# Shared FFN steps of the last tiles moved behind the constant tiles' indices

## What is computed

```python
def _ffn(x, gw, uw, dw):
    return jax.nn.silu(x @ gw.T) * (x @ uw.T) @ dw.T
shared = _ffn(xf, shared_gate, shared_up, shared_down)      # 704 hidden features, every token
probs = jax.nn.softmax(xf @ gate_w.T, axis=-1)
topw, topi = jax.lax.top_k(probs, 2)                        # 2 of 8 experts for each token
topw = topw / (topw.sum(-1, keepdims=True) + 1e-20)
routed = sum over experts of _ffn(xf, expert) * the token's weight for it
x = x + _layernorm(attention(_layernorm(x)))
x = x + _layernorm(shared + routed)
```

## Time and profile before

| | us |
|---|---|
| three runs, median (lowest to highest) | 841.98 (841.88 to 842.23) |
| the profiled execution, its own time | 840.84 |
| its span | 839.1 |
| TensorE busy in it | 783.3 |
| VectorE busy | 588.7 |
| ScalarE busy | 487.4 |
| GpSimd busy | 277.0 |

### The profile page before, as it was taken

How to read it: one execution, slowest core, us unless ns; L and a number is a source line. 1 busy time by engine, 2 the same in 40 slices (tenths; PEclk the granted TensorE clock), 3 DMA queues, 4 the chain that set the end, 5 groups by cost and what they waited for, 6 DMA issues and landing times.

```text
span 839.1 us, 21195 instructions
## 1 busy us (share of the span) xinstructions
PE 783.3 (93%) x6686; PEld 642.8 (77%) x6695; DVE 588.7 (70%) x1568; ACT 487.4 (58%) x1073; POOL 277.0 (33%) x301
## 2 busy tenths in 40 slices
PE   6989999999999997778999999999999999999990
PEld 3547777777777776666888888888888888888880
DVE  5758989898989898897888644555555555555552
ACT  3364848484857576533466655565656565656561
POOL 3011010101010101002565555555555555555542
PEclk9999999999999999999999999999999999999996
DMA  4114444444444343203264567856464646464633
GB/s 194 51 36 172 113 145 114 145 122 153 119 148 129 132 115 130 45 14 90 53 171 77 98 70 72 123 96 131 76 152 72 148 69 151 74 147 68 147 39 94
DMA packets 102708, 90.11 MB, mean 107 GB/s; under 512 B 63776, under 2 KB 94240, under 8 KB 101472
## 3 DMA queue, kind: packets, MB, share of 16 engines
q1 hardware_dynamic: 87664, 68.45, 28.7%
q0 software_dynamic: 14976, 20.78, 17.5%
HBM read 48.70 MB, written 27.39 MB: 91 GB/s over the span
## 4 chain that ended last, share of the span: by engine, by line
PE 73%; DVE 15%; issue 5%; ACT 5%; POOL 1%; DMA 1%; ACTq 0%; DVEq 0%; POOLq 0%
PE ps L948 41%; PE ps L963 19%; PE ps L1067 4%; PE ps L1099 3%; DVE wgu L1355 3%; DVE hf L1295 2%; PE ps L1061 2%; ACT wgu L805 2%; DVE wdn L1355 1%; DVE st L1537 1%; DVE att L1462 1%; PE ps L1028 1%; DVE hT L1305 1%; DVE st L1275 1%; PE ps L1070 1%
## 5 line engine op out<-in xcount | busy, mean ns | idle before, releaser
L948 PE MATMUL ps<-xhl,wgu 128*128 128x256 f16 x3102 | 383.6, 273 | 7.0 <-DVE hf L1295 5.2
L948 PEld LDWEIGHTS ps<-xhl,wgu 128*128 (+1 forms) x3102 | 301.8, 98 | 50.4 <-DVE hf L1295 6.8
L1295 DVE SCALAR_TENSOR_TENSOR hf<-ps,sc,silu 128x256 f32<-128x256 f32 x330 | 159.7, 484 | 172.4 <-ACT silu L755 146.2
L963 PE MATMUL ps<-wdn,hT 128*128 (+1 forms) x1870 | 253.3, 273 | 11.3 <-DVE hT L1305 8.5
L755 ACT ACTIVATE silu<-ps,sc 128x256 f32<-128x256 f32 x275 | 130.0, 473 | 226.2 <-PE ps L948 223.0
L963 PEld LDWEIGHTS ps<-wdn,hT 128*128 128x128 f16 x1870 | 180.9, 98 | 38.0 <-DVE hT L1305 7.6
L696 POOL DMA_INDIRECT acc_d<-ysb,gst x78 | 128.6, 1649 | 44.5 <-POOL gst L692 30.9
L641 POOL TENSOR_TENSOR rstd<-ve,mhalf 128x4 f32<-128x4 f32 (+1 forms) x32 | 30.7, 959 | 294.2 <-DVE ve L1280 272.5
L769 ACT CAST hT<-hf 128x256 f16<-128x256 f32 x275 | 109.7, 399 | 12.1 <-DVE hf L1295 10.1
L1305 DVE TENSOR_TENSOR hT<-hf,hT 128x256 f16<-128x256 f32 x275 | 114.8, 417 | 1.7
L685 POOL DMA_INDIRECT attw<-xn_d,gst x74 | 75.9, 1025 | 42.1 <-POOL gst L681 30.9
(11 more groups left out here) (242 smaller groups left out, 775.3 us busy)
## 6 DMA issues: line engine op xcount, KB each, us to landing
wgu<-in_gu SPq DMA_DIRECT2D x8, 1408.0 KB, 6.2
att<-in_x SPq DMA_DIRECT2D x16, 512.0 KB, 5.6
wdn<-in_dn SPq DMA_DIRECT2D x8, 768.0 KB, 8.2
x_d<-att SPq DMA_DIRECT2D x8, 512.0 KB, 2.9
xn_d<-wgu SPq DMA_DIRECT2D x8, 512.0 KB, 3.4
acc_d<-ysb SPq DMA_DIRECT2D x16, 256.0 KB, 3.3
att<-x_d SPq DMA_DIRECT2D x8, 512.0 KB, 4.8
att<-acc_d SPq DMA_DIRECT2D x7, 512.0 KB
```

Source lines behind the costliest of these rows:

```text
L948: ins = te.matmul(o, slot_gu(slot, hw, k, j), x(hx, k), start=(n == 0), stop=(n == len(TERMS) - 1))
L963: ins = te.matmul(y_bank(u, tt), h(hh), slot_dn(slot, c, hw), start=(c == 0 and n == 0 and tt == 0), stop=(c == FC - 1 and n == 1 and tt = ...
L1295: v.scalar_tensor_tensor(out=hf[lo:P, c % 2 * TW:(c % 2 + 1) * TW], in0=up, scalar=scale_of(slot, 1, lo, P), in1=silu[lo:P, c % 2 * TW:(c ...
```

## The change

Only the list `TAIL` is changed, the order of its steps. Nothing is added or taken away. Before, the H steps 5, 6 and 7 stood each behind a pair of `one_lo` steps or behind `one_hi` 1, all ahead of `route_indices`. Now `one_lo` 2 to 7 and `one_hi` 1 stand together, H 5 is behind `one_hi` 1, and H 6 and 7 are behind `route_indices`. D 4, G 7, D 5 and G 8 move behind the inversions with them. The heart of the diff:

```diff
-        ("G", 7), ("H", 6), ("D", 5), ("invert", 2), ("invert", 3), ("one_lo", 6), ("one_lo", 7), ("one_hi", 1), ("G", 8), ("H", 7),
...
+        ("G", 6), ("invert", 2), ("invert", 3), ("one_lo", 6), ("one_lo", 7), ("one_hi", 1), ("H", 5), ("invert", 4), ("invert", 5), ("invert", 6), ("invert", 7),
+        ("route_indices", 0), ("D", 4), ("G", 7), ("H", 6), ("D", 5), ("G", 8), ("H", 7), ("D", 6), ("G", 9), ("H", 8), ("D", 7), ("route_counts",), ("G", 10),
```

More of the change, by code:

```diff
@@ L82 @@
         ("H", 2), ("D", 1), ("route_slots", 1), ("one_lo", 1), ("route_weights", 1), ("G", 4), ("H", 3), ("D", 2), ("route_positions", 1), ("one_hi", 0),
[2 rows of a table removed]
-        ("invert", 4), ("invert", 5), ("invert", 6), ("invert", 7), ("route_indices", 0), ("D", 6), ("G", 9), ("H", 8), ("D", 7), ("route_counts",), ("G", 10),
+        ("G", 5), ("H", 4), ("D", 3), ("one_lo", 2), ("one_lo", 3), ("invert", 0), ("invert", 1), ("one_lo", 4), ("one_lo", 5),
+        ("G", 6), ("invert", 2), ("invert", 3), ("one_lo", 6), ("one_lo", 7), ("one_hi", 1), ("H", 5), ("invert", 4), ("invert", 5), ("invert", 6), ("invert", 7),
+        ("route_indices", 0), ("D", 4), ("G", 7), ("H", 6), ("D", 5), ("G", 8), ("H", 7), ("D", 6), ("G", 9), ("H", 8), ("D", 7), ("route_counts",), ("G", 10),
         ("H", 9), ("D", 8), ("G", 11), ("H", 10), ("D", 9), ("H", 11), ("D", 10), ("D", 11), ("route_segments",), ("route_order",)]
```

## The result

| | before | after |
|---|---|---|
| median of the timed runs, us | 842.11 (841.88 to 842.43, 4 runs) | 847.95 (847.31 to 848.98, 4 runs) |
| profiled execution, its own time | 840.84 | 848.98 |
| its span | 839.1 | 847.2 |
| start of the big `one_hi` (VectorE, L1454) | 361.35 | 364.51 |
| from there to L1149 (TensorE) | 25.91 | 31.12 |

The changed kernel is slower: ratio 1.007, 95% interval 1.0053 to 1.0088. That is 5.8 us, where 4.8 was forecast, and 0.15 us above the upper end of the range. The lower half of the table splits the span of the two profiles at an instruction shortly ahead of the change and at the product that closes the stretch: the change costs 31.12 - 25.91 = 5.2 us there by these two profiles, and nothing is made good behind it. The 3.2 us ahead of the change are no part of it; what they are is a question of its own (e5, e9).

A forecast was written before the change was run, and what follows sets the result against it. VectorE was taken as the limit up to the indices, then a chain across VectorE, ScalarE and TensorE. Hidden indices -0, later shared steps +3.3 and low clock +1.5 gave +4.8 us on 841.98: 846.8 us, range 844.4 to 847.8.

The forecast's parts named there:

- The clock's term: TensorE's D 4, G 7 and D 5: lower clock after a stretch of little work costs 1.5 us, bounded by 0 and 2.4.
- the sum: Indices -0, D 4 to hf 7 at full clock +3.3, low clock +1.5: +4.8 us, added to the median 841.98.
- The indices come earlier: VectorE's indices start at 372.55 instead of 374.35, 1.8 us earlier; no gain, hidden by the order of the tiles.
- the wait of 1.22 us ahead of G 0: TensorE's wait between the last filler matmul and the first routed G, taken as a wait for tile 0's tokens.
- Rival 3: Routed part: tokens bind, so it begins up to 1.2 us earlier, 840.8 us; soaked up or token-bound within 0.2%, 11%.
- The shared steps at full clock: D 4, G 7, D 5, tile 14's copies and silu 7 in a row: hf 7 at 376.9, not 373.62, 3.3 us later.
- Rival 2: Low clock lasts longer, through G 8 and D 6: +0.8, so 5.6 us later, 847.6 us; chance 6%.
- From D 6 to the order: Instructions and waits from D 6 to the order of the tiles stay as before: 12.6 us.
- "Some 2 us" for L1149's wait: Sign that the forecast is right: L1149 waits for VectorE near 392, some 2 us behind the routed G 0's end.
- rival 1: Clock kept by the inversions' matmuls, or falls where nobody waits: only +3.3 us, 845.3 us; chance 22%.

The follow-up runs named there:

- e5: The kernel before once more, no edit, profiled: 843.13 us, ratio 1.0007.
- e9: The kernel before, with useless matmuls in TensorE's waits ahead of the last list: 843.96 us, ratio 0.9986, on another chip where before takes 845.18.
- e7: The changed kernel with `route_indices` 0 moved behind H 7, so the indices are late: 847.02 us, ratio 1.0048 to before.
- e2: The changed kernel with useless 512-column matmuls put behind inversions 3 to 7: 846.44 us, ratio 1.0057 to before.
- e3: The changed kernel with ScalarE's two copies of tile 14's result moved behind silu 7: 846.11 us, ratio 1.0054 to before.
- e1: The changed kernel once more, no edit: 848.08 us, ratio 1.0065 to before at 842.50 us on the same chip.
- e4: The changed kernel with H 5, D 4 and G 7 back where they stood before the change: 847.11 us, ratio 1.0059 to before.
- e6: The changed kernel with both the edits of e2 and e3: 844.81 us, ratio 1.0026 to before.
- e8: The kernel before with another order of the same steps, only H 7 of H 5 to H 7 behind the indices: 841.74 us, ratio 0.9991.

## Why the prediction was wrong

The direction, the place and the chain were right; the size was short by 1.0 us, and the range ended 0.15 below the measured median. Two steps failed. The clock's term was 0.4 too small; that alone would have left the result in the range. The other 0.6 lies outside the stretch that the sum covers: the prediction put what is ahead of the change at nothing, and there the profiles of the changed kernel are 3.2 us behind the first one of before and 1.5 behind e5. Why the timed runs differ by 0.6 there stays open.

- **The indices come earlier**: 1.8 us forecast, 13.0 - 11.3 = 1.7 measured, and hidden, as said. e7 shows it. That G 0 would not wait for its tokens even with the indices 7 us later was not foreseen: the wait of 1.22 us ahead of G 0 was read as a wait for tokens in every execution. Its row says only `issue`, so that it was for the tokens is not shown, and e5 has none, though its G 0 starts 4.1 us behind the start of its transposes (382.55), against 5.5 in the earlier trace rows. Rival 3 rested on it and falls; hf 7, which it wanted by 373.6, came 5.3 later.
- **The shared steps at full clock**: 3.3 us forecast for hf 7. In e2 hf 7 starts 16.1 us behind the big `one_hi`, 15.7 without the 0.4 of the fillers, against 12.3 before: 3.4. The copies of tile 14's result are part of it: on hf 7 they and the wait for D 5 are 1.6 in e3 (at the lower level), on the distance 1.2; the working had 0.32 + 0.72 for the copies alone. The step that the diff does not show was the right one to look for.
- **The clock, the step that failed inside the stretch.** Of "Its cost is bounded by 0 below (clock kept) and by 2.4 above" I took 1.5, from one stretch of 3.4 us at the lower level as in the earlier trace rows. The lower level held from 373.8 to 380.7, twice as long, and began 2 us ahead of D 4 and not with it: D 4, G 7 and D 5 lie in it entirely. They took 4.67 us instead of 2.40, near the upper bound. Half a microsecond of that is hidden, because at full clock D 5 would have waited for its low half (377.73 + 0.56 = 378.3, where G 7 would have ended by 377.8). On hf 7 it came to 5.3 - 3.4 = 1.9, as e2 gives it, so 1.5 was 0.4 too little. Rival 2 had a longer lower level, but put it behind D 5, onto G 8 and D 6, and not ahead of D 4. What misled were two rows of a single execution. The 3.4 us are one: around D 3, where the two kernels are still alike, the lower level lasts 3.4 us in the profiles of before and e1 and 6.8 in e5 and e9. The idle time of 3.25 us that "did not lower it" is the other: in e5 the clock is down behind it.
- **From D 6 to the order**: 12.6 forecast, 395.57 - 383.05 = 12.5 measured. That the indices between hf 7 and hf 8 "had no part in it" is true of the first profile to 0.1 us; in e5 it takes 13.0, the 0.3 of the late indices with it, and so the stretch costs 31.1 - 26.2 = 4.9 us against e5 and 4.7 against e9. That these are so near to 4.8 is luck: the clock's 0.4 too little meets a delay in the kernel before that the rows did not have. "Some 2 us" for L1149's wait was a slip, the working's own numbers give 1.3 (383.23 + 1.30 + 1.35 + 4.8 = 390.7 against 392.0), and 1.27 was measured. All of the delay is carried to the end: 451.8 and 451.6 us from L1149 on.
- **The sum against a median.** 4.7 to 5.2 us is what the stretch costs in the profiles; the runs give 5.8 and, in e1's group, 5.6. In the profiles the rest lies in front of the change, where nothing was edited; for the timed runs that is likely and not shown. The working added its sum to a median of three runs (841.98) whose own kernel gives 842.5 with more runs (e1, e5) and scatters from 840.3 to 844.2. The lower level falls near 50 in some executions and near 334 in others, at 1.5 us each; both profiles of the changed kernel (first and e1) and e7 have it at both places, e4 and e6 near 50 alone, e2, e3, e5 and e8 near 334 alone, the profile shown of before at neither. The mean granted clock of that profile, 0.987, is rare: of 36 timed runs of before on two chips 4 have it, the others 0.979 to 0.983 (e5: 0.983). Whether the change brings the lower level to these places more often can't be told from so few profiles. A range for a difference on this kernel needed half a microsecond more on each side for that.
- **The clock was not kept** (rival 1). Of the 48 matmuls of the inversions, all between 371.1 and 375.3, 40 had run when it fell at 373.8; with the 512-column fillers of e2 between them it stayed at 1.00 from 372 to 378. The Trainium skill's rule (TensorE: Matmul & The Clock Gate, Part 1), read by the word idle, would have kept the clock, for 3.3 us in all. The changed kernel's windows decide against that reading.

## What to carry to other kernels

Before a step is moved, list what the same step issues on every engine, and what stands behind it in their queues: here two copies on ScalarE, harmless for as long as another engine was the limit, came onto the path by a move that did not touch their row. When a move takes an engine's lead away, its idle time can gather in one place; here TensorE's clock went with it, just when its work became the path. A thing made earlier is worth only as much as the last of the waits that it feeds: indices 1.7 us earlier were worth zero, because the order of the tiles, made by the same engine, was later. And before a number of a few microseconds is taken from one profile, a second profile of the same kernel is worth having: two rows that the clock's term rested on read differently in it.

## What the runs showed of the hardware

- The same kernel, unchanged ahead of the change, reached the big `one_hi` at 361.35, 363.0, 364.44 and 364.51 us in four profiles, by where the lower clock level fell. In e9, where matmuls without a use filled TensorE's waits, the timed runs of the kernel before went down by 0.14%.
- The same wait ends with the clock at either level, and the lower level lasts for different times. Behind the wait of 3.25 us near 350, the same code took 1.48 us in the first profile (clock 1.00) and 2.74 in e5 and e9 (0.50). Around D 3 of the last list the lower level lasted 3.4 us in the profiles of before and e1, and 6.8 in e5 and e9; in e5 TensorE was busy without a pause through the last 6.2 us of these.
- 40 matmuls of 16 columns in 2.7 us, in which TensorE was otherwise idle, did not keep the clock. The lower level then lasted some 6.8 us, well into dense work: G 7 took 2.56 us instead of 1.31.
